# A causal linear-attention encoder with its weight loads, weight splits and statistics put in another order

## The reference

```python
q, k, v = x @ Wq[l] + bq[l], x @ Wk[l] + bk[l], x @ Wv[l] + bv[l]      # 16 heads of 16
a = causal_linear_attn(elu(q) + 1, elu(k) + 1, v)     # masked scores in chunks of 128, plus a running sum
x = layer_norm(x + a @ Wo[l] + bo[l], g1[l], be1[l])
y = gelu(x @ W1[l] + b1[l]) @ W2[l] + b2[l]           # 256 -> 1024 -> 256
x = layer_norm(x + y, g2[l], be2[l])
```

## Time and profile before

| | before |
|---|---|
| median of 3 runs | 1584.66 us (1584.60 to 1586.51) |
| the profiled execution | 1584.66 us, its span 1582.9 us |
| PE busy | 1494.5 us (94%) |
| DVE busy | 1274.8 us (81%) |
| ACT busy | 994.2 us (63%) |
| POOL busy | 995.9 us (63%) |

### The profile page before, as it was taken

One profiled execution on the slowest core, in us unless ns is written; L12 is line 12 of the kernel. 1 busy time (PEld: TensorE's weight loads), 2 busy tenths in 40 slices (PEclk: granted clock), 3 DMA queues, 4 the chain that ended last, 5 costly groups with the idle time before them and its releaser, 6 DMA issues.

```text
span 1582.9 us, 38661 instructions
## 1 busy us (share of the span) xinstructions
PE 1494.5 (94%) x16086; PEld 1181.4 (75%) x16086; DVE 1274.8 (81%) x2190; ACT 994.2 (63%) x1608; POOL 995.9 (63%) x704
## 2 busy tenths in 40 slices
PE   4699999999999999999999999999998999999998
PEld 3588888888888888888887888878886566666434
DVE  4778888889888889888888888898775888888456
ACT  4465666666667666666666566756554777777445
POOL 5255767766777666776667676666586476763434
PEclk8899999999999999999999999999998999999999
DMA  6120011100111000210012000102033444443001
GB/s 137 38 65 19 18 25 38 58 25 19 25 47 57 17 19 25 68 41 15 15 34 86 25 12 11 48 15 50 2 72 119 138 148 134 143 136 89 1 1 54
DMA packets 99918, 82.53 MB, mean 52 GB/s; under 512 B 24608, under 2 KB 87968, under 8 KB 99744
## 3 DMA queue, kind: packets, MB, share of 16 engines
q1 hardware_dynamic: 99744, 80.06, 17.9%
HBM read 50.79 MB, written 14.68 MB: 41 GB/s over the span
## 4 chain that ended last, share of the span: by engine, by line
PE 70%; DVE 17%; ACT 4%; POOL 4%; issue 3%; DMA 1%; SPq 1%; ACTq 0%; DVEq 0%; POOLq 0%
PE e_pr L175 8%; PE e_pr L176 7%; PE e_pr L177 7%; PE e_sc L407 5%; PE e_tr L430 4%; PE x_psO L1441 4%; PE e_sc L175 3%; PE e_sc L176 3%; PE e_sc L177 3%; PE e_tr L175 3%; PE e_tr L176 3%; PE e_tr L177 3%; DVE e_qx_lo L891 3%; PE e_tr L425 2%; PE f_bank L1987 2%
## 5 line engine op out<-in xcount | busy, mean ns | idle before, releaser
L737 POOL TENSOR_TENSOR e_h_lo<-e_h_f,e_h_hi 128x512 fp32r<-128x512 f32 x192 | 262.9, 1377 | 198.0 <-ACT e_h_hi L553 195.4
L552 ACT ACTIVATE e_h_f<-e_pr,e_h_bias 128x512 f32<-128x512 f32 x192 | 131.9, 687 | 225.8 <-PE e_pr L177 220.5
L844 DVE TENSOR_TENSOR e_am<-e_sc,c_amask 128x1024 f32<-128x1024 f32 x192 | 225.7, 1216 | 51.9 <-PE e_sc L407 51.9
L175 PE MATMUL e_tr<-e_W_hi,e_h_hi 128*128 128x256 f32 x576 | 166.4, 289 | 9.9 <-DVE X L801 9.0
L1751 DVE TENSOR_REDUCE x_mx<-x_psS 128x4 f32<-128x1024 f32 x128 | 150.8, 1218 | 28.4 <-PE x_psS L1404 27.5
L175 PE MATMUL e_pr<-e_yT_hi,e_W_hi 128*128 128x512 f32 x384 | 167.4, 436 | 2.1 <-ACT e_h_hi L553 2.1
L176 PE MATMUL e_tr<-e_W_lo,e_h_hi 128*128 128x256 f32 x576 | 163.8, 284 | 0.0
L177 PE MATMUL e_tr<-e_W_hi,e_h_lo 128*128 128x256 f32 x576 | 163.5, 284 | 0.0
L176 PE MATMUL e_pr<-e_yT_lo,e_W_hi 128*128 128x512 f32 x384 | 151.9, 396 | 0.0
L177 PE MATMUL e_pr<-e_yT_hi,e_W_lo 128*128 128x512 f32 x384 | 151.8, 395 | 0.0
L1577 ACT ACTIVATE x_ex<-x_psT 128x1024 f32<-128x1024 f32 x128 | 130.9, 1022 | 25.8 <-PE x_psT L1426 20.9
(11 more groups left out here) (285 smaller groups left out, 4444.4 us busy)
## 6 DMA issues: line engine op xcount, KB each, us to landing
e_raw_m<-in_L_attn_W_dram SPq DMA_DIRECT2D x12, 1024.0 KB, 5.3
x_qs<-query_rows SPq DMA_DIRECT2D x48, 256.0 KB
e_x_raw<-e_x_blocks SPq DMA_DIRECT2D x368, 32.0 KB, 1.9
x_ks<-key_rows SPq DMA_DIRECT2D x48, 128.0 KB, 2.7
query_rows<-x_q_hi SPq DMA_DIRECT2D x16, 256.0 KB, 2.3
query_rows<-x_q_lo SPq DMA_DIRECT2D x16, 256.0 KB, 2.4
x_ctok<-in_ctx_dram SPq DMA_DIRECT2D x8, 256.0 KB, 3.4
x_xo<-in_x_dram SPq DMA_DIRECT2D x8, 256.0 KB, 3.1
```

Of the source, the lines that this page charges most:

```text
L175: pe.matmul(out, stat[0], mov[0], start=first, stop=False)
L552: act.activation(h_f[:, m % HR, :], ps_pr[m % 2][:, :], ACT.Gelu, bias=h_bias[:, m:m + 1])
L737: pool.tensor_tensor(h_lo[:, m, :], h_f[:, m % HR, :], h_hi[:, m, :].bitcast(F32), ALU.subtract).then_inc(h_lo_done, 1)
L844: dve.tensor_tensor(am[:, s % 2, c, :, :, :], ps_sc[:, :, c * 2 * P:(c + 1) * 2 * P].rearrange("p r (h n) -> p r h n", n=P), amask[:, :].u ...
```

## The change

Nothing is computed otherwise; instructions and loads stand at another place in their engine's list.

- SP: in the step with q = 0 (l > 0) W2 is loaded after `move_x` and no longer before it. bo of the next layer is loaded in the step with q = 2, after `move_x` and bv, and no longer in the step with q = 1.
- ACT: the four copies that make W1's high part stood at the end of the step with q = 3; now they stand in the step with q = 0 after `ktok`. In the last step `normed(2)` stands after gelu(3) as in the others, and no longer after gelu(7).
- GpSimd: W1's low part stands after `k_lo` in the step with q = 0, and no longer before `rsqrt(1)`. In the last step `gained(2)` and `shifted` stand before the items of the cross attention.
- VectorE: in every step `attn_lo(1)` stands before all four pairs of `residual(1, s)` and `spread(1, s)`; before, residuals 0 and 1 stood ahead of it and their two `spread` behind. In the last step but one `encoder_stats(0)` stands before `attn_lo(1)`.

```diff
--- before.py
+++ after.py
@@ -235,20 +235,17 @@
 
             def step(l, q, u, attn, mlp, following):
                 more = l < L - 1
-                if l > 0 and q == 0:
-                    sp.wait_ge(w1_lo, l + 1)
-                    load_w2(l)
                 if following:
                     move_x(u + 2)
                 if l > 0 and q == 1:
                     sp.wait_ge(ln_done[2], NT * l)
                     load_rows(l, ["g2", "be2"], rows_m, ln2_rows_loaded)
-                if more and q == 1:
-                    sp.wait_ge(xbo_done, NT * l + NT)
-                    load_rows(l + 1, ["bo"], rows_a, bo_loaded)
                 if q < 0:
                     sp.wait_ge(w1_lo, 1)
                     load_w2(0)
+                if l > 0 and q == 0:
+                    sp.wait_ge(w1_lo, l + 1)
+                    load_w2(l)
                 if more and q == 0:
                     sp.wait_ge(qkv_lo, l + 1)
                     load_attn_weights(l + 1, ["Wq", "Wk", "Wv"], raw_qkv_loaded)
@@ -259,6 +256,8 @@
                 if more and q == NT - 2:
                     sp.wait_ge(vx_done, 2 * (NT * l + NT))
                     load_rows(l + 1, ["bv"], rows_a, bv_loaded)
+                    sp.wait_ge(xbo_done, NT * l + NT)
+                    load_rows(l + 1, ["bo"], rows_a, bo_loaded)
                 if more and q == NT - 1:
                     sp.wait_ge(xb2_done, NT * l + NT)
                     load_rows(l + 1, ["g1", "be1"], rows_a, ln1_rows_loaded)
@@ -581,6 +580,11 @@
                     act.wait_ge(raw_qkv_loaded, 48 * (l + 2))
                     act.wait_ge(v_full, 2 * t + 2)
                     w_qkv(l + 1)
+                if l > 0 and q == 0:
+                    act.wait_ge(raw_1_loaded, 16 * (l + 1))
+                    act.wait_ge(h_full, FC * u)
+                    w_m("W1", w1_hi, 0)
+                    w_m("W1", w1_hi, 1)
                 if q == NT - 1 and attn:
                     act.wait_ge(raw_o_loaded, 16 * (l + 2))
                     act.wait_ge(wo_full, SB * t)
@@ -612,7 +616,7 @@
                         w_m("W1", w1_hi, 1)
                     if mlp:
                         gelu(2 + s)
-                    if s == 1 and u > 0 and attn:
+                    if s == 1 and u > 0:
                         normed(2, u - 1, (q - 1) % NT)
                     if following and s in (1, 2):
                         x_hi(t + 1, s - 1)
@@ -626,15 +630,8 @@
                 if mlp:
                     gelu(6)
                     gelu(7)
-                if u == final:
-                    normed(2, u - 1, (q - 1) % NT)
                 if attn:
                     attn_hi(1)
-                if more and q == NT - 1:
-                    act.wait_ge(raw_1_loaded, 16 * (l + 2))
-                    act.wait_ge(h_full, FC * u + FC)
-                    w_m("W1", w1_hi, 0)
-                    w_m("W1", w1_hi, 1)
 
             steps(step)
             cross.items()
@@ -690,22 +687,17 @@
                     add_row(0, rows_a["bo"], xT_tr, 2, bo_loaded, 16, xbo_done)
                 if u == final:
                     cross.encoder_scale(0)
-                if q == 0 and l > 0:
-                    w_m("W1", w1_hi, l, w1_lo, 0)
-                    w_m("W1", w1_hi, l, w1_lo, 1)
                 if mlp:
                     rsqrt(1, u)
-                    if u == final:
-                        cross.encoder_add(0)
-                    elif u > 1:
+                    if u > 1:
                         gained(2, u - 2, (q - 2) % NT)
                     gained(1, u, q)
-                    if u == final:
-                        cross.x1_norm(0)
-                        cross.keys_lo(0)
-                        gained(2, u - 2, (q - 2) % NT)
                     if u > 1:
                         shifted(u - 2, (q - 2) % NT)
+                if u == final:
+                    cross.encoder_add(0)
+                    cross.x1_norm(0)
+                    cross.keys_lo(0)
                 if attn:
 
                     for c in range(KC):
@@ -714,7 +706,7 @@
                     a.then_inc(k_lo_done, 1)
                 if q < 0:
                     w_o(1)
-                if q < 0:
+                if q < 0 or (q == 0 and l > 0):
                     w_m("W1", w1_hi, l, w1_lo, 0)
                     w_m("W1", w1_hi, l, w1_lo, 1)
                 if more and q == NT - 2:
@@ -998,25 +990,21 @@
                     reciprocals(1)
                     divide(1)
                     to_features(1)
-                    residual(1, 0, t, ta, wo_full, xbo_done)
-                    residual(1, 1, t, ta, wo_full, xbo_done)
                 if u == final:
                     cross.x1_transposed(0, cross.early(1))
                     cross.queries_hi(0, 0, cross.early(2))
                     cross.queries_lo(0, 0, cross.early(2))
+                if u == final - 1:
+                    dve.wait_ge(ln_done[2], final - 2)
+                    cross.encoder_stats(0)
                 if attn:
                     attn_lo(1)
                 if u == final - 1:
-                    dve.wait_ge(ln_done[2], final - 2)
-                    cross.encoder_stats(0)
                     cross.blocks()
                 if attn:
-                    spread(1, 0, t, ta)
-                    spread(1, 1, t, ta)
-                    residual(1, 2, t, ta, wo_full, xbo_done)
-                    spread(1, 2, t, ta)
-                    residual(1, 3, t, ta, wo_full, xbo_done)
-                    spread(1, 3, t, ta)
+                    for s in range(SB):
+                        residual(1, s, t, ta, wo_full, xbo_done)
+                        spread(1, s, t, ta)
                     moments(1, t)
 
             steps(step)
```

## The result

The kernel after the change takes 1673.71 us (median of 4 runs, 1672.36 to 1675.83), the one before in the same session 1585.59 us (1584.60 to 1587.27): a ratio of 1.0556, 95% interval [1.0537, 1.0574]. It is slower by 88 us. The forecast was 1680 us in a range from 1644 to 1706.

What follows compares the result with a forecast made beforehand. TensorE, busy 94% of the span, was taken to bound the kernel, so only its waits count. Terms 52.5 + 11 + 24 + 0 + 2.5 + 5 = 95 us on 1584.66 gave 1680 us, 6% slower, range 1644 to 1706.

Steps and rivals of the forecast that it cites:

- bo, stall: Five q = 2 steps: bo lands late behind move_x, holding GpSimd, normed(2) and TensorE about 10.5 us each, 52.5 us.
- bo, clock: After the q = 2 wait before mlp_up(6), TensorE restarts at half clock: 2.2 us a time, 11 us in all.
- W2: Five q = 0 steps: W2, issued behind move_x, lands late and holds ACT's copies and gelu(4): 24 us, clock included.
- W1's move: Layer boundaries, q = 0: earlier rsqrt(1) shrinks the 1.76 us wait, but W_lo slows qx_lo; zero by itself.
- VectorE's order: All 24 encoder steps: moments(1), and through it residual(2,2), come 0.44 us later; 2.5 us in all, from 0 to 9.
- end of the encoder: Last step: gained(2) and shifted ahead of encoder_add on GpSimd make x1_stats late; 5 us slower, from 0 to 8.
- Rival 1: After the q = 2 stall the low clock costs nothing, and W2's lateness is mostly hidden: some 1645 us, chance 13%.
- 0.25 us later: At q = 0, residual(2,2) and the transposes behind it come 0.25 us later, with qx_lo beside W_lo; counted under W2.

Runs made afterwards that it cites:

- 60 transposes: The kernel after the change plus 60 transposes of the unit matrix, never read, on TensorE ahead of mlp_up(6) in five q = 2 steps: 1663.60 us, ratio 1.0490.

## Why the prediction was right, step by step

The parts alone add up: 3.42 + 1.36 + 0.02 + 0.27 + 0.53 = 5.60% against 5.56% for the whole. In us, predicted and measured:

| term | predicted | measured |
|---|---|---|
| bo, stall | 52.5 | 44.5 (5 x 8.9) |
| bo, clock | 11 | 10 (5 x 2.0) |
| W2 | 24 | 22 alone, 17 beside W1's move |
| W1's move | 0 | 0 alone |
| VectorE's order | 2.5 | 4 |
| end of the encoder | 5 | 8 alone, 6 in the trace after |
| clock behind the transposes at q = 0 | in no term | about 5 where W2 is early, 0 where it is late |

- **bo.** The mechanism was right at each link: bo behind 16 moves and bv, GpSimd idle for 15.0 to 16.6 us (predicted 16.4), normed(2) 8.8 to 10.5 us later in its step than before (10.4), TensorE idle 6.7 to 8.3 us before mlp_up(6) (8.6). The term was mis-sized at its start and its end. In the step shown the moves did not begin 0.44 us later, they took 10.68 us and not 11.23, and bo landed in 4.5 us and not 4.8, so it came 1.3 us sooner than reckoned (0.75 on average over the five); only the step with the longest landing was as forecast. normed(2) was 9.4 us late on average, for 10.4. And in the run with 60 transposes, where the clock is kept up, normed(2) came 8.9 us late on average and the next rsqrt(1) 8.4, against the kernel with both loads back: the chain gave back 0.5, where I had it lose 0.1. The second wait, before mlp_up(7), was 0.54 us and not 2, because TensorE did mlp_up(6) at half speed; at full clock it was 1.80.
- **The clock.** 2.2 us a step forecast, 2.0 measured, from 0 to 2.6. Rival 1, by which a clock at half speed costs nothing here, falls with the 60 transposes: without the low clock the time is 10 us shorter. It held in one step of five.
- **W2.** The path was right and the sum of 24 us close to the 22 measured, but by luck: its two parts were both mis-sized and made good for each other. I had 3.3 us of stall a time, with ACT's copies beginning 24.6 us into the step. Moved alone, W2 came later, and the copies began at 25.0 to 26.5 after a wait of 4.9 to 6.4 us (4.6 forecast). That is about 21 of the 22 us. The clock, for which I had 1.5 us a time, cost about 1 us in all: from the start of the copies to the next mark it is 28.9 us in three steps, one without half clock and two with 3.4 us of it, and 29.6 us in the two with 6.8. Beside W1's move W2's price is smaller (2.13 - 1.06 = 1.07%, 17 us), since a late W2 hides the half clock behind the transposes for yT. With bo ahead of the moves and W2 late, the copies begin 29.3 to 29.4 us ahead of the next mark in four steps, two with that half clock and two without it. With W2 early it costs 1.5 us each of the four times that it comes.
- **W1's move.** That the 1.76 us would go, a pair of qx_lo would take 3.1 us beside W_lo and nothing would be won: right, with 3.11 us. Its "0.25 us later" hid a wait of 2.17 us before the transposes for yT that I did not name. It stands where one of 0.45 us stood, and the 1.76 us ahead of it are gone. And move_x, which I had 0.28 us later at q = 0, began 0.2 us sooner.
- **VectorE's order.** The step failed in its path. I had it come through residual(2, 2), whose wait of 0.7 us at q = 2 did not change at all. It came through qk(2)'s wait for residual(1, 2) of the step before, a wait that had no idle time before the change, so that it showed in no view. The size, 4 us instead of 2.5, was within my 0 to 9, by luck as far as the path goes.
- **The end.** x1_stats came 5.3 us later in its step, as reckoned (1175 for 1169.73). Its price is that of TensorE's wait behind it (6.08 us for 0.40) and half clock for 6.8 us. I had also counted on x1_norm, keys_lo and the keys' transfer behind them; that transfer lies on the chain that ended last before the change and no longer after it, so nothing shows that it had a part.

The sum came out 6 us above the time: 8 us too much for bo's stall, 1 for its clock and 2 for W2, less the 1.5 us that VectorE's order and the 3 that the end took more. Rival 1's own sum is a little off: 62 us more than before are 1647 us, not 1645.

## What to carry to other kernels

A transfer's time begins where its issue stands in the queue. Before a load is moved "a little later", count what is issued ahead of it and ask what event those wait for; here 16 small transfers waited for the same event as the user of the load. Where two engines slow each other, as VectorE's pair of qx_lo and GpSimd's W_lo do here (3.1 us for 1.4), place the movable work where the other engine is idle, in pieces if need be. Look for waits that are satisfied just in time, as qk(2)'s here: they have no idle time, so no view of waits shows them, and only the code does.

## What the runs showed of the hardware

- One issue of `move_x` on SP's queue took 0.64 to 0.70 us in the rows shown (10.19 to 11.23 us for 16), while the load of bo right behind them took 0.43: the length of one kind of issue doesn't tell that of another.
- The same wait at the same place of TensorE's list, 2.14 to 2.20 us before the transposes at q = 0, was followed by half clock in 1 of 5 steps in one kernel, 2 of 5 in another and 4 of 5 in a third, each time for 3.4 us and at 1.5 us of time. Where W2 is late the same half clock cost nothing. What decides whether it comes the runs don't show. A wait near 2 us thus has a price that changes from kernel to kernel: at five such places up to 7.5 us, 0.5%, for a part that changes nothing else.
- With the waits of 6.5 to 8.3 us before mlp_up(6) half clock came in 10 of 10 steps (the kernel after and the one with bo alone). It began before the end of the wait and lasted 6.8 to 13.7 us.
